# Edge counts spread over the base products: eleventh tile to the last base, one or two behind each product

## The reference, cut to what matters

```python
edge_index = jnp.stack([src, dst])
h = jnp.maximum(_layernorm(x), 0.0)
# layer 0, relational: message = (h @ weight[etype])[src] * edge_weight1, summed by dst,
#                      weight[r] = sum over 8 bases of w_comp[r, b] * bases[b]
x = x + L0(h, bases, w_comp, h_bias, edge_weight1, src, dst, edge_type_32)
h = jnp.maximum(_layernorm(x), 0.0)
# layer 1, two GCN convolutions: self loops, deg = number of edges into a node + 1,
#          norm = rsqrt(deg[src]) * rsqrt(deg[dst]), out = segment_sum((h @ W)[src] * norm) + b
x = x + L1(h, edge_index, W1, b1, W2, b2)
h = jnp.maximum(_layernorm(x), 0.0)
# layer 2: messages from edge attributes, spherical terms, summed by src
x = x + L2(h, src, dst, edge_attr_20, edge_weight, edge_attr_4, ...)
h = jnp.maximum(_layernorm(x), 0.0)
# layer 3, two SAGE convolutions: segment_sum(x[src]) / max(deg, 1) @ W_l.T + x @ W_r.T + b
return x + L3(h, edge_index, W1_l, W1_r, b1, W2_l, W2_r, b2)
```

## Time and profile before

| | |
|---|---|
| median of 3 runs | 1577.9 us (1575.59 to 1578.49) |
| the profiled execution | 1579.06 us, its span 1577.2 us |
| TensorE matmul busy | 1462.6 us, 93% of the span |
| VectorE busy | 993.9 us, 63% |
| ScalarE, GpSimd busy | 328.9 us (21%), 887.9 us (56%) |
| products with the bases, line 1148 | 311.6 us busy, 640 records |
| counts, line 1129, TensorE | 313 records |
| adds to `cnt`, line 1500, VectorE | 99.5 us busy, 313 |
| mean granted TensorE clock | 0.985 of full speed |

### The profile page before, as it was taken

How to read it: one execution, slowest core, us unless ns; L and a number is a source line. 1 busy time by engine, 2 the same in 40 slices (tenths; PEclk the granted TensorE clock), 3 DMA queues, 4 the chain that set the end, 5 groups by cost and what they waited for, 6 DMA issues and landing times.

```text
span 1577.2 us, 24690 instructions
## 1 busy us (share of the span) xinstructions
PE 1462.6 (93%) x6784; PEld 941.4 (60%) x6785; DVE 993.9 (63%) x2781; ACT 328.9 (21%) x806; POOL 887.9 (56%) x932
## 2 busy tenths in 40 slices
PE   4888888888889999999999998999999988999999
PEld 2777777777754444433447576666666655566465
DVE  8766666666666888898633333888888873421111
ACT  7000000000000000000062223555555545411100
POOL 5677777777722777677667761777777760000000
PEclk9999999999999999999999998999999998999999
DMA  4676666776765223422411111322222230000000
GB/s 159 192 198 199 192 203 201 203 202 199 200 173 164 78 74 92 136 83 70 125 61 25 26 28 62 105 72 64 72 65 70 68 54 1 28 0 1 27 34 34
DMA packets 91857, 159.19 MB, mean 101 GB/s; under 512 B 18747, under 2 KB 46960, under 8 KB 91792
## 3 DMA queue, kind: packets, MB, share of 16 engines
q0 software_dynamic: 42832, 103.15, 23.3%
q1 hardware_dynamic: 33728, 29.73, 6.0%
q10 hardware_dynamic: 15232, 25.52, 5.4%
HBM read 140.63 MB, written 17.70 MB: 100 GB/s over the span
## 4 chain that ended last, share of the span: by engine, by line
PE 52%; issue 15%; POOL 14%; DMA 12%; DVE 3%; ACT 1%; POOLq 1%; SPq 1%; DVEq 0%; ACTq 0%
PE ps L1148 14%; PE ps L935 12%; POOL u L801 11%; DMA gath<-h_rows,idx 10%; PE ps L923 9%; PE ps L878 8%; PE ps L1110 4%; POOL gath L740 3%; DMA u<-u_rows,at 2%; PE ps L1129 2%; PE ps L914 1%; PE ps L973 1%; DVE et L1299 0%; PE ps L1085 0%; DMA wc_blk<-in_w_comp_dram 0%
## 5 line engine op out<-in xcount | busy, mean ns | idle before, releaser
L878 PE MATMUL ps<-spread,gath 128*128 128x128 f32 x2504 | 354.9, 290 | 55.1 <-DMA gath<-h_rows,idx 43.8
L766 POOL DMA_INDIRECT slots<-att,idx_s x313 | 313.0, 1000 | 117.2 <-issue 92.9
L878 PEld LDWEIGHTS ps<-spread,gath 128*128 128x128 f32 x2504 | 306.5, 195 | 103.3 <-issue 59.5
L740 POOL DMA_INDIRECT gath<-h_rows,idx x313 | 300.3, 960 | 109.5 <-issue 58.8
L1148 PE MATMUL ps<-base_t,z 128*128 128x512 f32 (+1 forms) x640 | 311.6, 613 | 1.8 <-ACT z L527 1.0
L801 POOL DMA_INDIRECT u<-u_rows,at x243 | 239.1, 984 | 109.7 <-issue 70.7
L1361 DVE TENSOR_TENSOR z<-z,ps 128x512 f32 x313 | 215.0, 687 | 84.1 <-PE ps L878 69.1
L935 PE MATMUL ps<-hs,adj 128*128 128x512 f32 (+3 forms) x400 | 165.5, 414 | 0.0
L1038 PE MATMUL ps<-msg,hot 128*128 128x256 f32 x648 | 158.0, 388 | 6.4 <-DVE msg L1716 5.4
L935 PE MATMUL ps<-hl,adj 128*128 128x512 f32 (+3 forms) x400 | 157.6, 394 | 0.0
L1038 PEld LDWEIGHTS ps<-msg,hot 128*128 128x128 f32 x648 | 120.8, 192 | 56.5 <-DVE msg L1716 36.2
(11 more groups left out here) (264 smaller groups left out, 1678.3 us busy)
## 6 DMA issues: line engine op xcount, KB each, us to landing
base_t<-in_bases_dram ACTq DMA_DIRECT2D x64, 256.0 KB, 2.7
slots<-zero_t SPq DMA_DIRECT2D x6, 896.0 KB, 6.0
at<-slots SPq DMA_DIRECT2D x21, 256.0 KB
att<-in_attr_dram SPq DMA_DIRECT2D x79, 64.0 KB
gath<-h_rows,idx POOLq DMA_INDIRECT x313, 3.7
slots<-att,idx_s POOLq DMA_INDIRECT x313
u<-u_rows,at POOLq DMA_INDIRECT x243, 2.5
z<-in_x_dram SPq DMA_DIRECT2D x9, 256.0 KB, 5.1
```

The costliest lines, as they stand in the source:

```text
L740: nc.gpsimd.indirect_dma_start(out=gath[:, c % RING, :], out_offset=None, in_=h_rows, in_offset=bass.IndirectOffsetOnAxis(ap=idx[:, par, c ...
L766: nc.gpsimd.indirect_dma_start(out=slots, out_offset=bass.IndirectOffsetOnAxis(ap=idx_s[0:r, turn_of, at_quad * QUAD + c:at_quad * QUAD + ...
L878: last = mm(bank[:, k * P:(k + 1) * P], gath[:, h_slot, k * P:(k + 1) * P], s_of.rearrange("p b d -> p (b d)"), start=True, stop=True)
```

## The change: where the counts stand between the products

```diff
         RANK_PACE = HALF - 1
-        COUNTS, FIRST_COUNT = HALF + 2, BLOCKS
+        FIRST_COUNT = BLOCKS + 1
+        COUNT_SPAN = ((2 * BASES - 1) * KIN - FIRST_COUNT) * HALF
...
-        LOW_OCT, LOW_STEP = ((BASES + 2) * KIN + 3 - FIRST_COUNT) * COUNTS // OCT, 2
+        LOW_OCT, LOW_STEP = ((BASES + 2) * KIN + 3 - FIRST_COUNT) * HALF * REAL_CHUNKS // COUNT_SPAN // OCT, 2
...
-        assert FIRST_COUNT + -(-REAL_CHUNKS // COUNTS) <= (2 * BASES - 1) * KIN
...
             def rank_and_count(i):
...
-                tile, j = i // HALF, i % HALF
-                t = (tile - FIRST_COUNT) * COUNTS
-                if tile >= FIRST_COUNT:
-                    for c in range(t + j * COUNTS // HALF, t + (j + 1) * COUNTS // HALF):
-                        if c < REAL_CHUNKS:
-                            count(c)
+                at = i - FIRST_COUNT * HALF
+                if at >= 0:
+                    for c in range(at * REAL_CHUNKS // COUNT_SPAN, (at + 1) * REAL_CHUNKS // COUNT_SPAN):
+                        count(c)
```

## The result

| | before | changed |
|---|---|---|
| median, same chip | 1576.93 us (1575.59 to 1579.4, 6 runs) | 1583.99 us (1582.02 to 1586.32, 6 runs) |
| ratio to before | | 1.0038, 95% interval [1.0025, 1.005] |
| profiled execution, span | 1579.06 us, 1577.2 us | 1584.27 us, 1582.5 us |
| mean granted clock | 0.985 | 0.982 |

The changed kernel is 0.38% slower by the ratio on record; the quotient of the two medians is 1.0045, just as clearly above 1. The prediction was 1583.5 us, worked out from a median of 1577.9 for before. The same +5.6 us from the 1576.93 of these six runs would be 1582.5, so part of the closeness to 1583.99 is luck. The two profiled executions differ by 5.2 us, 1584.27 against 1579.06.

A forecast was written before the change was run, and what follows sets the result against it. TensorE was taken to bound the kernel between 455 and 786 us. Terms of -7.0 us until product 299, then exposed sums and slow clock, came to +5.6 us on the path: median 1583.5 us, range 1579.5 to 1588.6.

The forecast's parts named there:

- The start: At the first count, five more products ahead remove a 3.13 us wait and 1.7 us of slow clock: -4.8 us.
- The pace: Same 313 counts behind 245 products instead of 224; 21 turn from seconds of a pair into single ones: +1.0 us.
- VectorE's pauses: Five `take_low` pauses between the counts, 6.8 us before, stay at about 1.2 us each: -0.8 us.
- Pairs that wait: Pairs of counts whose second waits for VectorE's add, 3.6 us in all; two thirds go with wider spacing: -2.4 us.
- Until product 299: Sum of start, pace, pauses and pairs up to the end of product 299: -7.0 us.
- The end of the counts: Sums of `cnt`, hidden before, become exposed: `cnt_done` 23.9 us behind the last count, TensorE waiting 9.8 us at the degrees.
- The clock behind the wait: Low clock on the degrees and block 8's four products after TensorE's wait: 2.7 us taken, 5.8 as upper bound.
- +5.6 at block 8: Product 319, the last of block 8, ends at 791.4 instead of 785.78 us: +5.6 us on the path.
- all moves along: Everything behind product 319 shifts with it, since the norm of the next rows needs that product: +5.6 us kept.
- Cancelling: Rival: slower pace removes all pair waits and half the pauses, so gain and loss cancel: 1577.8 us; chance 0.17.
- Staying hidden: Rival: the sums end before TensorE reaches the degrees, so the whole -7.0 us stays: 1570.9 us; chance 0.05.
- The low clock that ends at +10.7: Rival: low clock holds through degrees, products and layer 1's first product: 1588.6 us; chance 0.12, shared with remaining count waits.

The follow-up runs named there:

- e3: The changed kernel with its first count behind product 50 instead of 55, still spread to product 299; ratio 1.0073 to before.
- e10: The changed kernel with counts spread over products 50 to 284, so the slower pace without the later start or late end; ratio 1.0000 to before.
- e4: The changed kernel with the two reductions of cnt replaced by two constant fills; ratio 0.9962 to before.
- e9: The changed kernel itself, run again on another chip; ratio 1.0023 [0.9996, 1.0050] to before.
- e11: The changed kernel with counts spread over products 55 to 284 instead of 55 to 299, third sample; ratio 0.9997 to before.
- e8: The changed kernel with the degrees moved behind the last product (319) instead of behind 315; ratio 0.9987 to before.
- e1: The kernel before with counts starting behind product 55 instead of 50, at the old pace of 7 counts to 5 products; ratio 0.9967 to before.
- e2: The changed kernel with counts spread over products 55 to 284 instead of 55 to 299, first sample; ratio 0.9975 to before.
- e6: Repeat of e1 on another chip: the kernel before with only the later start, behind product 55; ratio 0.9964 to before.
- e5: Repeat of e2 on another chip: the changed kernel with counts spread over products 55 to 284; ratio 0.9955 to before.
- e7: The changed kernel with 11 extra unread products between product 315 and the degrees, to fill TensorE's wait; ratio 0.9977 to before.

## Why the prediction was right, and what was mis-sized

- **What bounds the stage.** TensorE, until the degrees. Right: the two traces differ in it by TensorE's waits, the clock behind them and the pace.
- **The start, -4.8 us.** Right, and seen in the trace of after (508.45 without a wait, clock 1.00); e3 and e10 bring the 3.13 us back. The first count ran at 508.45 and not at 509.2 mostly because in this execution product 49 ended 0.6 us earlier, as did all ahead of it (GpSimd's memset starts at 501.41 and not at 502.04); that is scatter and no gain. The other 0.2 us was a slip of the prediction: a count starts at the pace of the starts, before the record ahead of it ends.
- **The pace, +1.0 us.** Right in its parts: single counts step by 0.97 us, products with a pair by 1.03.
- **VectorE's pauses, -0.8 us.** The direction held. By the same reading the five now cost 6.0 to 6.3 us (6.8 before), so it is -0.5 to -0.8.
- **Pairs that wait, -2.4 us.** Too small: 14 pairs waited before and 2 do now, so not two thirds but nearly all of it went, and what is left is some 0.3 us of the 3.6. The term is -3.3. VectorE, with its 0.77 us per count, catches up in nearly every case.
- **Until product 299, -7.0 us.** From the end of product 49's record to that of product 299, before took 765.9 - 504.9 = 261.0 us and the changed kernel 757.3 - 504.3 = 253.0: -8.0, of which the pairs are 0.9 of the missing 1.0.
- **The end of the counts.** The decisive step was right: `cnt_done` came 24.3 us behind the last pair (23.9 predicted), the wait was 9.41 us (9.8 predicted), and e4 shows that the sums alone make it. The margin of 12.7 us that before had was the whole protection.
- **The clock behind the wait, 2.7 us.** Too small: degrees 4.2 us by the distance of starts instead of 2.1, products 5.8 instead of 3.5, so 4.4 us on the first chip and 5.0 in e9. I had taken the value nearer to the start's 1.7, which followed a wait of 3.13 us with full products behind it; here the wait was three times as long and 20 records of one column came first, all of them at 0.50. Which of the two makes the difference was not separated. The upper bound of 5.8 for the whole piece held. The rule of the Trainium skill that was weighed ("TensorE: Matmul & The Clock Gate", Part 1: activity releases the clock, so an added wait is paid again behind it) led to 3.8 in the prediction, which was nearer than my 2.7 and still short of 4.4: of the four products nearly three ran slow and not two. The trace agrees with the rule that this is paid twice.
- **+5.6 at block 8.** Measured +5.85, as a sum of errors that cancel: 1.7 more for the clock and 0.4 for the sums, 0.9 less for the pairs, 0.6 less by scatter of the start, and some 0.3 less in smaller terms. That the sum is within 0.3 us is luck; the terms are off by up to 1.7.
- **Behind it "all moves along".** Roughly. The distance was 4.2 us at line 935 and 5.3 at the end. The 1.7 us less at line 935 is the low clock that before had at 790 to 794 us and the changed kernel had not. It is no property of the change: e9 takes 3.22 us for its first four records of line 923, and before 3.19, the changed kernel 1.88, as e10 and e11.
- **The rivals.** Cancelling needed `cnt_done` at 778.9; it came at 781.4. Staying hidden would have needed sums under 13 us; e4, which makes them short, has just that. The low clock that ends at +10.7 did not come on the first chip; e9 comes nearer to it (6.62 us for the products and a slow start of layer 1 behind them), and e8's clock at the start of layer 1 too, but no run reached it.

## What to carry to other kernels

Before moving the last instruction of a chain later, find what begins only with its end, here a reduction of 22.7 us over the whole tensor, and how long its reader takes to arrive: this slack (12.7 us), not the pace, is the budget of the spread. A first wait that can be passed by one tile of other work is a gain by itself, so take the two halves of such a change apart. Price an added TensorE wait with a piece of low clock behind it: here 1.7 us behind 3.13 with full products following, 4.4 to 5.0 behind 9.4 to 9.8 with one-column records following. Take a difference of 1.7 us behind a gap as scatter until it shows in two executions.

## What was not expected of the hardware

**The clock fell with TensorE in work.** In e1 and e2 nothing waited, the 20 degree records took 2.24 us, and the eight records behind took 5.38; the same kernels again (e6, e5, e11) gave 3.68. In e1:

```profile
1219.00:1221.00 2.00, 2.00 (x20) 1.99 (x19) 1.47 (x3) 0.00 (x0) 0.00 (x0) 1.00 0.00 0
1221.00:1223.00 2.00, 2.00 (x7) 1.01 (x7) 0.70 (x6) 0.91 (x2) 0.00 (x0) 0.78 0.00 0
1223.00:1225.00 2.00, 2.00 (x4) 0.85 (x3) 0.00 (x0) 0.10 (x1) 0.00 (x0) 0.50 0.00 0
```

TensorE is busy all along by the records; what came just before is a run of one-column matmuls. It happened in 2 of the 8 traces that reach the degrees without a wait, and in e7. Why in these and not in the others stays open.

**Chips on which instructions come late.** All three chips of the experiments are so. In e9's table of waits:

```profile
PEld ps L1129 <- issue: 445.2, 263, 9.0
DVE cnt L1498 <- remote: 321.4, 59, 8.4
```

and in two stretches, the first with GpSimd's scatters in it and the second without:

```profile
700.00:800.00 100.00, 35.49 (x72) 11.45 (x72) 18.00 (x84) 0.00 (x0) 70.48 (x77) 0.59 0.13 34
...
1060.00:1160.00 100.00, 94.59 (x313) 38.32 (x311) 83.23 (x379) 0.00 (x0) 0.00 (x0) 1.00 0.25 79
```

72 matmul records in 100 us. The changed kernel on the first chip has 330 with the same scatters beside them:

```profile
520.00:620.00 100.00, 98.98 (x330) 41.77 (x327) 80.46 (x383) 2.56 (x5) 71.03 (x78) 1.00 0.29 80
```

"issue" and "remote" name nothing that the profile shows, and no experiment was made on it; the cause is open.
